# Counting the edges: four groups of counts in eight PSUM banks, one-hots two groups ahead, two places read together

## The reference

```python
x = layernorm(x + gin(x, src, dst))      # 2 layers; each: agg = segment_sum(x[src], dst)
x = layernorm(x + mpnn(x, e, src, dst))  # messages from x[src], x[dst], e; segment_sum
x = layernorm(x + gin3(x, e, src, dst))  # 3 layers, batch norm over the edges
x = layernorm(x + sage(x, src, dst))     # 2 layers; each: agg = segment_sum(x[src], dst)
```

## Time and profile before

| What | Value |
|---|---|
| median of three runs | 4864.7 us |
| the profiled execution | 4827.65 us, its span 4826.2 us |
| the stage of counts | from 34.65 to 322.92 us of the span: 288.27 us |
| busy in the stage: DVE, ACT, PE | 244.81, 203.26, 173.18 us |
| mean granted TensorE clock in the stage | 0.60 |

### The profile page before, as it was taken

One profiled execution on the slowest core, in us unless ns is written; L12 is line 12 of the kernel. 1 busy time (PEld: TensorE's weight loads), 2 busy tenths in 40 slices (PEclk: granted clock), 3 DMA queues, 4 the chain that ended last, 5 costly groups with the idle time before them and its releaser, 6 DMA issues.

```text
span 4826.2 us, 57244 instructions
## 1 busy us (share of the span) xinstructions
PE 2815.5 (58%) x12415; PEld 1700.8 (35%) x12415; DVE 2115.7 (44%) x2957; ACT 1578.0 (33%) x3332; POOL 2134.1 (44%) x2027
## 2 busy tenths in 40 slices
PE   4667946776777444333687433335873433358797
PEld 1123434444444232222454222223542322235443
DVE  8876832233233533333673333335743333347601
ACT  6776222222222222222462222223632222236410
POOL 1005624544541355555463555554645555536200
PEclk7568965555555767667898677767996776769998
DMA  1002033333331355555484565554855565538500
GB/s 55 0 0 86 1 100 115 104 108 103 100 110 36 128 191 195 188 183 187 154 268 137 192 200 191 184 189 135 268 168 182 195 203 189 186 120 268 197 1 14
DMA packets 271498, 679.44 MB, mean 141 GB/s; under 512 B 48481, under 2 KB 81174, under 8 KB 270006
## 3 DMA queue, kind: packets, MB, share of 16 engines
q1 hardware_dynamic: 155574, 332.76, 21.7%
q0 software_dynamic: 73216, 190.95, 13.8%
q10 hardware_dynamic: 42624, 154.70, 8.5%
HBM read 502.27 MB, written 175.94 MB: 141 GB/s over the span
## 4 chain that ended last, share of the span: by engine, by line
PE 30%; another core or an unknown queue 25%; issue 20%; DVE 15%; ACT 4%; DVEq 4%; ACTq 1%; DMA 0%; POOL 0%; SPq 0%; POOLq 0%
PE psum L629 7%; PE psum L458 6%; PE psum L769 6%; DVE acc L1218 4%; PE psum L731 3%; PE psum L505 3%; PE psum L472 3%; DVEq L909 2%; DVE tN L1270 1%; DVE tN L1226 1%; DVE acc L922 1%; PE psum L565 1%; DVEq L402 1%; PE psum L733 1%
## 5 line engine op out<-in xcount | busy, mean ns | idle before, releaser
L769 PE MATMUL psum<-w_all,region 128*128 128x256 f32 x2496 | 830.8, 495 | 1307.3 <-ACT region L1472 751.8
L769 PEld LDWEIGHTS psum<-w_all,region 128*128 128x128 f32 x2496 | 598.0, 250 | 1539.9 <-issue 927.8
L382 POOL DMA_INDIRECT region<-tab,idx_ring x624 | 589.8, 945 | 783.7 <-issue 752.6
L382 POOL DMA_INDIRECT tN<-tab,idx_ring x624 | 589.9, 945 | 361.2 <-issue 188.0
L1226 DVE TENSOR_TENSOR region<-region,psum 128x1024 f32<-128x1024 f32 x156 | 190.2, 1219 | 938.1 <-remote 648.9
L1639 POOL TENSOR_TENSOR region<-node_no,dst_rel 128x256 f32<-128x256 f32 x312 | 384.2, 1232 | 324.3 <-ACT region L1516 241.0
L1486 ACT ACTIVATE psum<-region 128x1024 f32<-128x1024 f32 x156 | 160.2, 1027 | 911.0 <-DVE acc L1218 438.5
L1218 DVE TENSOR_TENSOR acc<-acc,psum 128x1024 f32<-128x1024 f32 x312 | 379.5, 1216 | 53.0 <-issue 30.7
L731 PE MATMUL psum<-w_all,region 128*128 128x128 f32 x832 | 326.3, 493 | 112.4 <-issue 74.0
L1226 DVE TENSOR_TENSOR tN<-tN,psum 128x1024 f32<-128x1024 f32 x156 | 190.2, 1219 | 436.1 <-remote 250.8
L382 POOL DMA_INDIRECT region<-tabs,idx_ring x208 | 201.8, 970 | 301.6 <-issue 301.6
(11 more groups left out here) (267 smaller groups left out, 4110.0 us busy)
## 6 DMA issues: line engine op xcount, KB each, us to landing
region<-e_t SPq DMA_DIRECT2D x416, 256.0 KB
pre_dram<-region ACTq DMA_DIRECT2D x144, 512.0 KB
pre_dram<-tN ACTq DMA_DIRECT2D x144, 512.0 KB
region<-pre_dram SPq DMA_DIRECT2D x144, 512.0 KB, 4.6
tN<-pre_dram SPq DMA_DIRECT2D x144, 512.0 KB, 4.5
tA<-dst_row SPq DMA_DIRECT2D x78, 256.0 KB
adj_kept<-region SPq DMA_DIRECT2D x5, 2000.0 KB, 15.1
region<-adj_kept SPq DMA_DIRECT2D x5, 2000.0 KB, 15.7
```

Of the source, the lines that this page charges most:

```text
L382: pool.indirect_dma_start(m_ring[j][:, c, at:at + width], None, table[:, :], bass.IndirectOffsetOnAxis(ap=idx_at(j, k)[:, c:c + 1], axis=0 ...
L769: mm = pe.matmul(banks[:, 2 * (j % 2) + c // 2, (c % 2) * 256:(c % 2) * 256 + 256], e_ring[:, j % E_SLOTS, c * D:(c + 1) * D], W(f"ee{l}") ...
```

## The change

PSUM: group j of a trip uses banks 2 (j mod 4) and 2 (j mod 4) + 1, so that all eight banks hold the counts of four groups. TensorE waits for the addition of four groups ago instead of two.

VectorE: before the loop it makes the one-hots of groups 0 and 1. In the loop, for each group g, it first reads both places of the group, then makes the four one-hots of group g + 2, then does both additions of group g. The order is the same for all groups of a trip. The loop has 12 trips; the last eight groups are written out behind it, the last two of them without one-hots.

```diff
 PRIMED = {... "adj_mm": 2 * KEY_SLOTS,
-          "adj_add": 4,
+          "adj_add": 2 * KEY_SLOTS,
@@ TensorE
-                        pe.wait_ge(S["adj_add"], T["adj_add"] + 2 * g + k - 3)
+                        pe.wait_ge(S["adj_add"], T["adj_add"] + 2 * g + k - (2 * KEY_SLOTS - 1))
                         for c in range(2):
-                            mm = pe.matmul(banks[:, 2 * (j % 2) + k, 0:ADJ_COLS], ...
+                            mm = pe.matmul(psum[:, 2 * slot + k, 0:ADJ_COLS], ...
@@ VectorE
-            def add_counts(g, j):
-                for k in range(2):
-                    start = dve.value_load(adj_at_i[0:1, bass.ds(2 * g + k, 1)], min_val=0, max_val=N_NODES - 1)
+            def key_hots(g, j):
+                dve.wait_ge(S["adj_mm"], T["adj_mm"] + 2 * (g + 1) - 2 * KEY_SLOTS)
+                for c in range(GC):
+                    last = dve.tensor_scalar(key_ring[:, j % KEY_SLOTS, c, :], key_no,
+                                             key[:, bass.ds(g * GC + c, 1)], None, ALU.is_equal)
+                last.then_inc(S["key_oh"], 1)
+
+            def count_group(g, j, ahead):
+
+                starts = [dve.value_load(adj_at_i[0:1, bass.ds(2 * g + k, 1)], min_val=0, max_val=N_NODES - 1)
+                          for k in range(2)]
+                if ahead:
+                    key_hots(g + 2, j + 2)
+                for k, start in enumerate(starts):
                     to = counts[:, :, bass.ds(start, ADJ_WIN)]
                     dve.wait_ge(S["adj_mm"], T["adj_mm"] + 2 * g + k + 1)
                     dve.wait_ge(S["adj_add"], T["adj_add"] + 2 * g + k)
-                    dve.tensor_tensor(to, to, banks[:, 2 * (j % 2) + k, 0:ADJ_COLS].rearrange("p (t d) -> p t d", t=N_TILES),
-                                      ALU.add).then_inc(S["adj_add"], 1)
+                    dve.tensor_tensor(to, to, psum[:, 2 * (j % KEY_SLOTS) + k, 0:ADJ_COLS].rearrange(
+                        "p (t d) -> p t d", t=N_TILES), ALU.add).then_inc(S["adj_add"], 1)
 
             dve.wait_ge(S["adj_zero"], 1)
-            with dve.Fori(0, TRIPS) as i:
-                for j in range(UNROLL):
-                    g = i * UNROLL + j
-                    (the wait and the four one-hots of group g, as in key_hots)
-                    if j:
-                        add_counts(g - 1, j - 1)
-                add_counts(g, j)
+            for g in range(2):
+                key_hots(g, g)
+            with dve.Fori(0, TRIPS - 1) as i:
+                for j in range(UNROLL):
+                    count_group(i * UNROLL + j, j, True)
+            for j in range(UNROLL):
+                count_group((TRIPS - 1) * UNROLL + j, j, j + 2 < UNROLL)
             count_first(T)
```

More of the change, by code:

```diff
@@ L60 @@
 PRIMED = {"sc_mm": UNROLL, "sq": UNROLL, "ve_mm": E_SLOTS, "ohT": E_SLOTS, "pre": UNROLL, "sc_add": 2,
-          "sq_add": 2, "adj_mm": 2 * KEY_SLOTS, "adj_add": 4, "win_out": 2, "win_t": 2}
+          "sq_add": 2, "adj_mm": 2 * KEY_SLOTS, "adj_add": 2 * KEY_SLOTS, "win_out": 2, "win_t": 2}
 ONE_BY_ONE = ["consts", "loaded_sp", "loaded_gam", "loaded_act", "setup_to_pe", "setup_to_dve", "lane_set", "loaded_idx", "windows_set",
@@ L605, in pe_program @@
                     for k in range(2):
-                        pe.wait_ge(S["adj_add"], T["adj_add"] + 2 * g + k - 3)
+                        pe.wait_ge(S["adj_add"], T["adj_add"] + 2 * g + k - (2 * KEY_SLOTS - 1))
                         for c in range(2):
-                            mm = pe.matmul(banks[:, 2 * (j % 2) + k, 0:ADJ_COLS], lane_ring[:, slot, 2 * k + c, :],
+                            mm = pe.matmul(psum[:, 2 * slot + k, 0:ADJ_COLS], lane_ring[:, slot, 2 * k + c, :],
                                            key_ring[:, slot, 2 * k + c, :], start=(c == 0), stop=(c == 1))
```

## The result

| | before | changed |
|---|---|---|
| median of six runs each | 4860.31 us (4847.35 to 4869.63) | 4942.87 us (4920.27 to 4956.11) |
| ratio | | 1.0164, 95% interval 1.0132 to 1.0195 |
| profiled execution | 4827.65 us | 4942.67 us, its span 4941.4 us |
| the stage of counts | 34.65 to 322.92, 288.27 us | 34.38 to 410.14, 375.76 us |
| the end of the stage | | 87.2 us later |

What follows compares the result with a forecast made beforehand. VectorE's sequencer, its place reads covered only by the second addition, was taken as the bound: 1.68 + 1.04 + 0.80 = 3.52 us a group, stage end 404.0 us (+81), 4946 us on the median; range 4895 to 4978.

Steps and rivals of the forecast that it cites:

- What bounds: Stage of counts: VectorE's sequencer and the cover of its 0.71 us reads set the pace, not the datapath alone or TensorE.
- The total: Whole kernel: the stage ends at 404.0 us, 81 us later, giving 4946 us on the median; chance 0.76.
- Eight banks, nothing: PSUM: TensorE no longer waits for the addition of two groups ago, worth nothing since VectorE sets the pace.
- One-hots two groups ahead: VectorE: removes 10.9 us of waits for TensorE and the emptied pipeline at trip boundaries (2.60 us where one-hots need 2.08).
- rival 2: VectorE: the wait for the first addition doesn't hold the sequencer; 2.60 us a group, -9 us, 4856 us; chance 0.05.
- Second addition to one-hots, 1.68 us: VectorE, second addition's start to next one-hot: two reads, 1.44 us, plus operations; 1.68 us where it was 0.60.
- rival 1: VectorE's sequencer: the two reads overlap in part, 0.34 us less a group, 3.18; +46 us, 4911 us; chance 0.10.
- First addition to the second, 0.80: VectorE, between a group's additions: 0.68 addition, 0.04 to the waiting operation, 0.09 to the next addition; 0.80 us, was 0.99.
- The last groups: Last eight groups, written out: 3.16 us for six, 2.15 for the two without one-hots, together 23.3 us.
- The rest of the kernel only shifted: Behind the stage of counts: the rest stays as it was, only later, so the kernel loses the stage's loss in full.
- Views: Profile: VectorE's idle time ahead of one-hots, about 1.0 us a group, labelled issue; between additions 0.31 falls to 0.12.
- Rival 3: VectorE: reads fully hidden, so its datapath bounds at 2.44 us a group; -28 us, 4836 us; chance 0.05.

Runs made afterwards that it cites:

- experiment 1: Changed kernel, but each place read just before its own addition: 2.62 us a group, stage ends at 312.63 us, median 4802.63 us, ratio 0.9975.
- experiment 5: Kernel before, but both places read together ahead of the next group's one-hots: 3.51 us a group, stage ends at 403.77 us, 4885.01 us (one run).
- experiment 6: Changed kernel, but two one-hots, read, addition, twice per group, in the loop: 2.61 us a group, stage ends at 310.55 us, 4803.93 us (one run).
- experiment 7: Changed kernel, but each read just before its addition and all 104 groups written out: 2.49 us a group, median 4797.60 us, ratio 0.9958.
- experiment 8: Changed kernel, but all groups written out, with two one-hots before each read and addition: 2.21 us a group, median 4758.61 us, ratio 0.9874.
- experiment 2: Kernel before with the eight banks alone: 2.62 us a group, stage ends at 320.98 us, 4818.16 us (one run).
- experiment 4: Changed kernel with one read less, one place used for both additions: 2.79 us a group, stage ends at 328.81 us, 4814.96 us (one run).
- experiment 9: Changed kernel unaltered, run again beside the kernel before: stage ends at 410.24 us, median 4946.66 us against 4854.37 us, ratio 1.0195.

## Why the prediction was right

- **What bounds.** Right, and shown by experiments 1, 5 and 6: the sequencer of VectorE, at 2.6 us for a group, and the cover of the reads, not the datapath and not TensorE. Experiments 7 and 8 confirm it: fewer operations of the sequencer give 2.49 and 2.21 us.
- **The total.** The stage lost 87.2 us where 81 were forecast. That 4946 us lies 3 us from the measured median, 4942.87, is in part luck: the kernel before had 4864.7 us in the forecast's three runs and 4860.31 in all six, and what lies behind the stage spreads by more than the 6 us.
- **Eight banks, nothing.** Right for the waits of TensorE, and 1.9 us earlier by themselves (experiment 2). What I left out is that they change the form of VectorE's waits, which costs 0.06 us a group in the changed kernel (below).
- **One-hots two groups ahead.** The emptied pipeline at the boundaries goes, as said. With the reads in place this, the banks and the written-out last groups are worth 10.3 us (322.92 to 312.63, experiment 1); rival 2 gave 9. The 10.9 us of waits for TensorE were misread in part: 13 of the 30 waits, 5.6 us, stand at the start of a trip, and belong to the same boundary as the 2.60 us. The other 17, of 0.31 or 0.32 us, lie between two additions like the one at 85.70, where the read was what took the time. No term of the sum used the 10.9.
- **Second addition to one-hots, 1.68 us.** Measured 1.66 to 1.69. The two reads cost twice one read, 0.71 each; rival 1, the overlap, is out by the chain and by experiment 4.
- **Four one-hots, 1.04.** Measured 1.04.
- **First addition to the second, 0.80.** Measured 0.86, the one term of a steady group that was mis-sized (its three parts add up to 0.81). I had the wait on the operation directly ahead of the addition, as in the kernel before. With the eight banks the wait for the first addition comes as an operation of its own (L923, at 89.84), and L924's (at 89.91) stands behind it. It isn't the order of the reads that does this: in experiment 5, with both reads first and four banks, the additions lie 0.79 to 0.80 apart and a group takes 3.51 us, which is the forecast's 3.52. 104 times 0.06 are 6.2 us, about the distance from the predicted end, 404.0, to the measured 410.1; what the other terms miss is small and nearly cancels.
- **The last groups.** 3.16 and 2.15 us were forecast, 3.17 and 2.28 measured, and one of them 3.55 by a stall. The 3.17 holds the 0.86 too, so what the constants save was a little more than I took off.
- **The rest of the kernel only shifted.** Right by the medians (experiment 9), though the profiled execution was 28 us longer behind the stage.
- **Views.** I expected the gap ahead of the one-hots to be named issue. It is named TensorE for 102.4 us: I had the size and the place but not the label. The idle time between the two additions fell to 0.19 us, where 0.12 was forecast, for the reason above.
- **Rival 3** asked for both reads to fit under what is queued, and nothing in the change did that. No run has both reads in a row fully hidden. With the reads apart and shorter, experiment 7 comes to 2.49 us, about the rival's 2.44 with 0.86 in place of 0.80, and experiment 8, where no addition waits for the one before, goes below it.

The Trainium skill (Perfetto Trace Analysis, "Per-engine timelines") has both kinds of waiting, an engine instruction's in a queue and a sequencer instruction's in the sequencer. In these loops the trace agrees with the second, as the operation that carries the wait belongs to the sequencer: in the chain above the first addition ends at 89.82, the waiting operation (L923) starts at 89.84, and the reads only come behind the second addition.

## What to carry to other kernels

A register read of a value from SBUF in an inner loop is a fixed piece of the sequencer's time, here 0.71 us, and is free only if as much engine work is queued in front of it: place each under its own cover (one under the one-hots, one under the addition), not two together (0.96 us a group lost ahead of the one-hots, 0.60 behind them, against experiment 1). Before moving waits or buffers, add up the sequencer's operations for one round; where their sum is the period, only fewer operations (constants instead of loop registers) make it shorter, and only then does the order of the engine's instructions count. And look through a long gap in the chain of waits before believing the releaser in brackets.

## What the runs showed of the hardware that I had not expected

- What a wait costs depends on where the compiler puts it. From the end of one addition to the start of the next that waits for it: 0.10 us where the waiting operation is the last ahead of the addition and does nothing else (experiment 4), 0.12 where it is the last and does register arithmetic too (experiment 5), 0.19 where another operation stands behind it (the changed kernel, and experiment 7 with constants).
- Code that runs for the first time stalls, and less so afterwards. Written out, VectorE's list stalls once in eight groups: its datapath loses 0.36 us with a nearly empty queue (experiment 7: 2.85 against 2.49) and 0.12 with work queued (experiment 8). In the loops one group of each trip stalls in the same way: in the first trip by 0.36 us (3.94 against 3.58 in the changed kernel, 3.00 against 2.64 in the kernel before), in each later one by 0.11 to 0.12. Writing out all 104 groups cost nothing beyond this stall.
- What lies behind the stage, with the same code in all ten kernels, took 4472 to 4543 us in the profiled executions, where the end of the stage repeated to 0.1 us.
